# One-hots of an embedding tower: ids in SBUF compared with row numbers in PSUM, two chunks per VectorE operation

## The reference, cut to what matters

```python
e = jnp.stack([tbl_0[ids[:, 0]], tbl_1[ids[:, 1]], ..., tbl_31[ids[:, 31]]], axis=1)   # (512, 32, 256)
dots = jnp.einsum('bnd,bmd->bnm', e, e)          # per sample, every pair of fields
z = dots[:, iu, ju]                              # the 496 pairs with i < j
h = jnp.concatenate([z, dense_ctx], axis=1)      # (512, 512)
h = jnp.maximum(h @ W_top1 + b_top1, 0.0)        # 512 x 512
h = jnp.maximum(h @ W_top2 + b_top2, 0.0)        # 512 x 256
y = h @ W_top3                                   # (512, 1)
```

## Time and profile before

| | |
|---|---|
| median of 3 runs | 162.0 us (161.57 to 162.75) |
| the profiled execution's own time | 162.26 us |
| its span, first to last instruction | 160.5 us |
| TensorE (PE) busy | 148.6 us, 93% |
| TensorE weight loads (PEld) busy | 130.2 us, 81% |
| GpSimd (POOL) busy | 104.0 us, 65% |
| VectorE (DVE) busy | 89.1 us, 56% |
| ScalarE (ACT) busy | 73.0 us, 45% |
| HBM read | 24.26 MB, 151 GB/s over the span |

### The profile page before, as it was taken

How to read it: one execution, slowest core, us unless ns; L and a number is a source line. 1 busy time by engine, 2 the same in 40 slices (tenths; PEclk the granted TensorE clock), 3 DMA queues, 4 the chain that set the end, 5 groups by cost and what they waited for, 6 DMA issues and landing times.

```text
span 160.5 us, 4781 instructions
## 1 busy us (share of the span) xinstructions
PE 148.6 (93%) x1974; PEld 130.2 (81%) x1974; DVE 89.1 (56%) x287; ACT 73.0 (45%) x178; POOL 104.0 (65%) x110
## 2 busy tenths in 40 slices
PE   6999999899999989988989999799989798998994
PEld 6788888788868868777869989699979797997972
DVE  0799976746847034998708644708554344353410
ACT  3356787484764336564340543603441505071421
POOL 1587777777878777777777777777777777700000
PEclk9999999999999999999999999999999999999999
DMA  4899989778655756953333433343333333310000
GB/s 122 239 346 361 371 286 285 206 242 223 186 164 183 204 192 228 267 162 107 102 98 112 118 104 102 101 117 110 103 101 108 115 111 98 102 35 4 4 0 5
DMA packets 11423, 24.58 MB, mean 153 GB/s; under 512 B 2757, under 2 KB 3209, under 8 KB 11402
## 3 DMA queue, kind: packets, MB, share of 16 engines
q0 software_dynamic: 4992, 13.64, 29.2%
q1 hardware_dynamic: 6266, 10.38, 19.9%
q10 hardware_dynamic: 144, 0.26, 0.6%
HBM read 24.26 MB, written 0.00 MB: 151 GB/s over the span
## 4 chain that ended last, share of the span: by engine, by line
PE 40%; POOL 32%; issue 15%; DMA 9%; ACT 3%; DVE 0%; POOLq 0%
POOL rows L345 32%; PE bank L614 11%; PE bank L608 11%; DMA rows<-table,row_ids 6%; PE bank L641 5%; PE xt_ps L580 5%; PE bank L560 3%; PE bank L668 2%; DMA first_sb<-first_ids 2%; ACT xt L461 1%; PE xt_ps L668 1%; PE bank L676 1%; ACT h L495 0%; PE xt_ps L676 0%; ACT h L487 0%
## 5 line engine op out<-in xcount | busy, mean ns | idle before, releaser
L345 POOL DMA_INDIRECT rows<-table,row_ids x104 | 103.4, 994 | 35.0 <-issue 29.0
L393 DVE COPY pairs<-bank 32x64 f32<-32x64 f32 (+1 forms) x184 | 39.6, 215 | 6.7 <-PE bank L608 2.2
L461 ACT COPY xt<-xt_ps 128x512 f32<-128x512 f32 (+1 forms) x44 | 23.0, 557 | 36.3 <-PE xt_ps L580 35.8
L608 PE MATMUL bank<-xt 128*64 128x64 f32 x1024 | 33.4, 223 | 3.6 <-ACT xt L461 2.5
L608 PEld LDWEIGHTS bank<-xt 128*64 128x64 f32 x1024 | 31.3, 138 | 6.5 <-ACT xt L461 3.7
L580 PE MATMUL xt_ps<-ident,rows 128*128 128x128 f32 x208 | 29.6, 277 | 4.1 <-DMA rows<-table,row_ids 3.9
L580 PEld LDWEIGHTS xt_ps<-ident,rows 128*128 128x128 f32 x208 | 23.1, 140 | 8.5 <-DMA rows<-table,row_ids 4.2
L364 DVE TENSOR_SCALAR one_hot<-small_ids_sb,first_sb 128x512 fp32r<-128x512 int32 x48 | 22.2, 493 | 10.1 <-PE bank L560 10.1
L560 PE MATMUL bank<-one_hot,high 128*128 128x512 f32 x96 | 26.5, 398 | 0.0
L375 DVE COPY xt<-xt_ps 128x512 f32<-128x512 f32 (+1 forms) x13 | 8.2, 630 | 32.2 <-PE xt_ps L580 32.2
L560 PE MATMUL bank<-one_hot,low 128*128 128x512 f32 x96 | 25.8, 391 | 0.0
(11 more groups left out here) (37 smaller groups left out, 41.3 us busy)
## 6 DMA issues: line engine op xcount, KB each, us to landing
small_sb<-small_tables SPq DMA_DIRECT2D x23, 256.0 KB, 5.1
w_sb<-w SPq DMA_DIRECT2D x8, 256.0 KB
rows<-table,row_ids POOLq DMA_INDIRECT x104, 3.7
small_ids_sb<-small_ids SPq DMA_DIRECT2D x5, 256.0 KB, 5.8
w_sb<-w SPq DMA_DIRECT2D x1, 512.0 KB, 5.9
small_ids_sb<-small_ids ACTq DMA_DIRECT2D x1, 256.0 KB, 3.7
small_sb<-small_tables SPq DMA_DIRECT2D x2, 128.0 KB, 3.5
ids_sb<-ids SPq DMA_DIRECT2D x1, 100.0 KB, 3.2
```

What stands on the lines that cost most here:

```text
L345: nc.gpsimd.indirect_dma_start(rows[:, i % ROWS, :], None, table, bass.IndirectOffsetOnAxis(ap=row_ids[:, i:i + 1], axis=0)).then_inc(gath ...
L393: done = nc.vector.tensor_copy(to, source)
L461: nc.scalar.copy(*fill_parts(f)).then_inc(xt_act, 1)
L608: done = nc.tensor.matmul(dots_ps[n % 2][quads, g, :], x, x, start=(c == 0), stop=(c == DC - 1))
```

## The change: row numbers to PSUM, one comparison for two chunks

Once, at the start, VectorE copies the row numbers (128 x 8) into the first 8 columns of `banks[4]` and waits for that copy. Then each two has one `tensor_tensor` that compares the ids (read twice, by a step of 0) with two row numbers per partition (each read 512 times), and writes both one-hots, 128 x 1024. Its wait for TensorE asks for both chunks of the earlier two. The rest of `prepare` is the same but for its indices: `low` is made as before.

```diff
+        chunk_rows_ps = banks[4][:, 0:CHUNKS]
...
+        chunk_rows_placed = sem("chunk_rows_placed")
...
+            nc.vector.tensor_copy(chunk_rows_ps, chunk_rows_sb).then_inc(chunk_rows_placed, 1)
+            dve.wait_ge(chunk_rows_placed, 1)
 
             def prepare(two):
-                for i in range(2 * two, 2 * two + 2):
-                    k, c = divmod(i, CHUNKS)
-                    if c == 0:
-                        dve.wait_ge(small_ids_in[k % TABLE_IDS], 16 * (k // TABLE_IDS + 1))
-                    if i >= ONE_HOTS:
-                        dve.wait_ge(chunk_used, i - ONE_HOTS + 1)
-                    nc.vector.tensor_scalar(one_hot[:, i % ONE_HOTS, :], small_ids_sb[:, k % TABLE_IDS, :],
-                                            chunk_rows_sb[:, c:c + 1], None, ALU.is_equal).then_inc(one_hot_ready, 1)
+                i = 2 * two
+                k, c = divmod(i, CHUNKS)
+                if c == 0:
+                    dve.wait_ge(small_ids_in[k % TABLE_IDS], 16 * (k // TABLE_IDS + 1))
+                if i >= ONE_HOTS:
+                    dve.wait_ge(chunk_used, i - ONE_HOTS + 2)
+                nc.vector.tensor_tensor(one_hot[:, i % ONE_HOTS:i % ONE_HOTS + 2, :],
+                                        small_ids_sb[:, k % TABLE_IDS:k % TABLE_IDS + 1, :].to_broadcast([KR, 2, B]),
+                                        chunk_rows_ps[:, c:c + 2].unsqueeze(2).to_broadcast([KR, 2, B]),
+                                        ALU.is_equal).then_inc(one_hot_ready, 2)
 
                 dve.wait_ge(high_ready, highs(two))
                 k %= TABLES
-                nc.vector.tensor_tensor(low[:, k, c - 1:c + 1, :], small_sb[:, k, c - 1:c + 1, :],
-                                        high[:, k, c - 1:c + 1, :], ALU.subtract).then_inc(low_ready, 1)
+                nc.vector.tensor_tensor(low[:, k, c:c + 2, :], small_sb[:, k, c:c + 2, :],
+                                        high[:, k, c:c + 2, :], ALU.subtract).then_inc(low_ready, 1)
```

## The result

The changed kernel takes 164.39 us (median of 5 runs, 163.36 to 166.89) against 161.74 of the kernel before in the same comparison: ratio 1.0145, 95% interval 1.0098 to 1.0193. It is slower by 1 to 1.5%. The medians here are of all executions; the ratios leave out those more than 1.5% above the fastest of the same kernel. One execution was profiled: 163.36 us, the fastest of the five, span 161.6.

The account below looks back on a forecast made before the run. TensorE and GpSimd share the bound; a lasting GpSimd delay moves the end one for one. Gather losses of 6.7 + 1.5 = 8.2 us against 4.9 make 3.3 more: 165.3 us against the median, range 161.0 to 167.5.

Parts of the forecast that it names:

- The comparison: VectorE's merged one-hot operation, 1024 columns with row numbers from PSUM: 1.22 us, bounds 0.87 and 2.1.
- The period: VectorE's steady stretch, merged one-hots plus `low` per two: 1.74 us in place of 1.39.
- The forecast's margin of 0.07: VectorE's next `low` starts 1.74 us after the last, the next gather 1.81 after it: 0.07 us between them.
- The chain of holds: GpSimd's gathers 6 to 17: each begins just after a `low`, is held, costs 0.49 us; 5.9 in all.
- What holds a gather: GpSimd beside VectorE: mainly `low`'s subtraction holds a gather beginning with it, until 0.56 us after `low` starts.
- the 4.9 us: GpSimd in the kernel before: gather time beyond 0.947 us each, over the first 11 and next 24 gathers.
- Rival 1: GpSimd's gathers: the old one-hots held them, so the change frees all 4.9 us; 158.6 us, chance 0.10.
- The start: TensorE's first lookup: one-hots come 0.9 us late, at 6.2; costs nothing while GpSimd is later, alone about 0.5.
- How far it goes: GpSimd's total delay: gathers 6 to 17 held, 8.2 us lost against 4.9, so 3.3 us later.
- Gathers 1 and 5: GpSimd's early gathers meeting a `low` before the steady repeat: about 0.36 and 0.40 us added.
- The late twos: Eight twos left at TensorE's pace after the steady stretch: gathers lose 1.5 us, ends 0.8 and 4.4.
- Free twos and the later wait: VectorE's wait for two used chunks: starts 0.45 us later with three twos in hand, costs nothing.

Follow-up runs that it names:

- The run with one SBUF input: Changed kernel, but `low`'s subtraction takes its second input from the row numbers in PSUM (for measurement alone): 157.79 us, ratio 0.9707.
- the spacer: Changed kernel plus one unused VectorE copy of 48 columns from PSUM per two, ahead of the comparison: 158.5 us, ratio 0.9756.

## Why the prediction was right, point by point

- **The comparison**, 1.22 us from the two copies out of PSUM: measured 1.215 (29.2 us over 24). The period, 1.74: 1.73. By the Trainium skill ("VectorE: DVE Perf Modes", The TRN2 errata) PSUM would have added 0.065; the trace disagrees: `low` with two SBUF inputs takes 0.68 for 512 columns, and by 0.53 more for the further 512 a comparison without any addition would take 1.21. The run with the merged comparison from SBUF shows it directly: the same 128x1024 took 1.220 on the mean with both inputs in SBUF and 1.215 with one in PSUM. The forecast's margin of 0.07 would have been all but used up by 0.065, and at a period of 1.80 the chain did break.
- **The chain of holds**: right, in place (from gather 6) and size (1.43 predicted as 1.44, 1.73 apart). Two of its sums are slightly off, without effect: 5 + 15 x 1.74 is 31.1, not 31.3, and 13.3 + 10 x 1.74 is 30.7, not 30.8. The run with one SBUF input and the spacer show it from both sides.
- **What holds a gather**: half right. I took the 4.9 us as mainly due to `low`. With `low` out of the way the old one-hots still held gathers about half as much in total, and locked them to the same period. The rows of the steady stretch before said so already: its gather at 12.31 begins 0.51 us after the `low` at 11.80, so a hold up to 0.56 explains 0.05 of its 0.14 us over 0.95, and the run in which `low` reads from PSUM has the same 1.09. That the old period of 1.39 was taken over because of `low` was in the main a wrong reading; that the new one would be, because the gathers then begin 0.07 after a `low`, was a right one. Rival 1 was wrong about the result and right about the part. By the Trainium skill ("SBUF — State Buffer", Who interferes with whom) both kinds can contend with GpSimd, and here gathers took 1.09 beside the old one-hots and 1.43 beside `low`; its inference that a DMA's descriptors don't suffer from an operation with two SBUF inputs does not carry over to these gathers, which took 1.43 to 1.98 beside such operations instead of 0.95. They also read their row numbers from SBUF, and no run separates that reading from the descriptors.
- **The start**: 5.35 to 5.97, with the first ids 0.26 us earlier in this execution, so 0.9 as said, and hidden as said.
- **How far it goes**: this term was mis-sized. 12 held gathers were forecast, and 10 came in the first profile, where VectorE's 15th two waited 0.21 us for TensorE and the chain broke; in the three further profiles in which VectorE's program is that of the changed kernel 12 came. Gathers 1 and 5 were put at 0.36 and 0.40 and cost 0.18 and 0.36. The late twos were put at 1.5 us (0.8 to 4.4); in the first profile they cost about 0.8. So the gathers' busy time rose by 1.2 us there, by 1.8, 2.2 and 3.0 in the others (105.2, 105.6 and 106.4 against 103.4), where I had 3.3. The time followed one for one, as the prediction had it for a delay of GpSimd: against the 162.26 of the profiled execution before, these four took 1.1, 1.6, 2.0 and 2.8 us longer. By the medians it is 164.1 to 164.5 instead of 165.3.
- **Not foreseen**: the half clock after TensorE's longer waits. The prediction had the waits, near 31 to 36 us, but gave them no further price; it is about 0.8 us by the medians, and may be nothing.
- **Free twos and the later wait** for two used chunks: nothing in the trace speaks against their price of nothing.

## What to carry to other kernels

Where two engines contend and neither waits for the other by a semaphore, don't price a contention by averages: compare the period of the one with the step of the other, and ask where the next meeting falls. A shorter or a longer loop may both be better than one that just repeats the meeting; 0.07 us less per two (1.73 for 1.80) cost 2% of the whole, and 0.12 us more gave 3.5% back. And before moving one operand of one operation to PSUM, look which other operation beside it still has two inputs in SBUF.

## What the runs showed of the hardware that was not expected

- A VectorE operation with one SBUF and one PSUM input, of 512 or 1024 columns, held no gather; with two SBUF inputs of 512 columns it held each one that began 0.05 to 0.5 us after its start, until about 0.56 us after that start: gathers took 1.46 at a lead of 0.05, 1.43 at 0.08, and in the first profile of the changed kernel 1.31 at 0.18 (11.39 after 11.21) and 1.13 at 0.38 (6.21 after 5.83). A gather that began within 0.03 us won with 0.95 (in that profile 47.40 after 47.37), and VectorE's operation took 0.72 to 0.75 for 0.68.
- TensorE's granted clock fell to 0.50, its lower level of 1.2 GHz, about 1 us after it had taken up work again following waits of 1.28 and 2.55 us, and stayed there for over 3 us; with matmuls in the waits it stayed at 1.00. In the first profile, with one wait of 1.24 us at that place, it stayed at 1.00 as well.
- Two one-hots of 512 columns from SBUF took 0.87 together in the kernel before and 0.75 after a pause on VectorE. Why is open.
